# Two 16-head attentions of a layered network: heads in groups side by side, outputs turned, smaller decay tables

## The chip, the cores and the metric

The kernel runs on one core of one Trainium2 chip. The metric is the device time of one execution in microseconds (us). The kernel before takes 3792.23 us, the median of three runs (3791.14 to 3802.96).

## The reference

The network has four levels of self attention, cross attention and feed forward, twelve stages on x (4 batches, 256 tokens, 256 channels, float32), each `x = x + stage(layernorm(x))`. The change rewrites the first two stages.

The first attention is linear attention over 16 heads of 16 channels, with a decay per head, in chunks of 128 tokens:

```python
D = jnp.exp(ld[:, None, None] * jnp.where(mask, diff, 0)) * mask
q_decay = jnp.exp(ld[None, :] * (idx + 1)[:, None])
k_decay = jnp.exp(ld[None, :] * (chunk - 1 - idx)[:, None])
scores = jnp.einsum('bchd,bshd->bhcs', qb, kb) * D[None]
o_intra = jnp.einsum('bhcs,bshd->bchd', scores, vb)
o_inter = jnp.einsum('bchd,bhde->bche', qb, S) * q_decay[None, :, :, None]
```

q, k and v are silu(x W). The output times the sigmoid of a gate (x Wg1 Wg2) is normalised per head by its root mean square, multiplied by norm_w and by Wo. The first cross attention has 16 heads of 16 channels too, keys and values from a latent of 64 channels, a causal mask over 256 x 256 and a softmax.

## The kernel before, in words

A stage is a run of blocks; in a block each engine has its own list of instructions, they wait for each other through semaphores, and a block ends in a barrier. `layernorm` (L203) turns the normalised x into xnT, with channels down the partitions. `refine_rsqrt` (L185) makes one Newton step of four VectorE instructions; all 12 layer norms use it, and two stages. `load` (L314) issues loads on the SyncE queue in the order of its list, and `wait_weights` waits for all loads of one name. A float32 matmul of 128 rows appears in the trace as two records of TensorE (PE) and two weight loads (PEld); a transpose as one.

`l0_attn` (L331) has four blocks. The first (L360 to L461) loads everything under one name and waits for it, then projects q, k and v into PSUM banks: 12 steps through six banks, then the gate's two products. ScalarE takes tanh or silu, VectorE finishes q and k, with q kept twice, once with the odd heads cleared (L425) and once with the even ones (L424), so that 32 rows of k (two heads) can meet one head of q. After that ScalarE makes the table of decays, Exp per head at L457 and Ln at L460, and VectorE corrects it (L430, L433), squares it three times (L435 to L437) and masks it (L438): 16 heads x 384 columns = 6144.

The second block has a loop over 4 x 16 heads. Per head TensorE makes scores in two matmuls of 32 rows (L476 with 256 columns, L478 with 128) and, two heads later, the sums over keys in three matmuls with 128 x 128 weights and 16 columns:

```python
nc.tensor.matmul(o[:, 0, cols], p[:, 0:P], v[:, 2 * b, cols], start=True, stop=True)
nc.tensor.matmul(o[:, 1, cols], p[:, 2 * P:3 * P], v[:, 2 * b + 1, cols], start=True, stop=False)
nc.tensor.matmul(o[:, 1, cols], p[:, P:2 * P], v[:, 2 * b, cols],
```

VectorE multiplies scores by the table (L507). The third block normalises over all tokens at once (L525 to L535, refined at L532), and `project_out` (L256) transposes the result and multiplies it by Wo.

`l0_xattn` (L545) projects in its first block (L579 to L605) and then loops over 32 pairs of heads: scores (L626, L628), mask added by VectorE (L672), maxima (L677 to L679), Exp with its sum on ScalarE (L719), six transposes (L638), a copy (L686), and the sums over keys in 12 records of 16 columns (L651 to L653); `project_out` ends it.

Three other places serve for comparison. In the three latent cross attentions L1569 makes scores with 64 rows for j = 0 and 1 in rows 0 to 63 and 64 to 127, and L1591 writes its results to PSUM partitions 0 to 63 and 64 to 127 in turn; L1579 transposes. In the last self attention L2268 makes scores with 32 rows, two for each of two neighbouring groups of 32 rows. L1223 belongs to the second level's attention.

## Time and profile before

| | |
|---|---|
| profiled execution | 3792.42 us |
| its span in the profile | 3790.2 us |
| TensorE busy | 2875.6 us, 76% |
| VectorE busy | 1894.3 us, 50% |
| ScalarE busy | 1018.8 us, 27% |
| GpSimd busy | 780.8 us, 21% |
| DMA | 73.06 MB, 19 GB/s over the span |
| mean granted TensorE clock | 0.782 of full speed |

The clock is given as a share of 2.4 GHz; 0.50 is 1.2 GHz. The busy shares are means over twelve stages with different limits, so they say little about the two stages at hand; those are read from stretches of time. Column "(x)" counts instructions.

### The profile page before, as it was taken

The numbers are of one execution on the slowest core, as the hardware profiler recorded it, in microseconds if no ns is written. First come the engines' busy times: TensorE is split into PE (matmuls) and PEld (weight loads), VectorE is DVE, ScalarE is ACT, GpSimd is POOL, SyncE is SP. The second block draws the span as 40 slices with busy tenths as digits, with TensorE's granted clock in tenths as the row PEclk, the third lists the DMA queues.
The fourth block names the chain that finished last, engine by engine and source line by source line (L and its number), as shares of the span: only waits on it lengthen the run. The fifth ranks groups of instructions, "written<-read, shape, count | busy, mean of one in ns | idle before, by whom it ended". The sixth has DMA issues, their size and how long they took to land. (4 is left out here: it accounts for less than half of the span.)

```text
span 3790.2 us, 37772 instructions
## 1 busy us (share of the span) xinstructions
PE 2875.6 (76%) x14229; PEld 1963.0 (52%) x14230; DVE 1894.3 (50%) x3700; ACT 1018.8 (27%) x2426; POOL 780.8 (21%) x531
## 2 busy tenths in 40 slices
PE   4596995343649999977768787875999665599799
PEld 2485884221223335555566666664555644455455
DVE  3523444586953345533657575753355645155521
ACT  3000321011520025511233334331355201045411
POOL 0000002000210038821100000000487000068522
PEclk8556555555759999988778787877899875699999
DMA  1000000000020000012000000003000000300211
GB/s 38 0 1 15 1 1 28 5 0 3 0 82 0 0 1 1 1 46 84 18 12 12 12 12 12 12 12 78 1 1 1 34 16 1 78 1 1 64 46 42
DMA packets 95934, 73.06 MB, mean 19 GB/s; under 512 B 50672, under 2 KB 89249, under 8 KB 95178
## 3 DMA queue, kind: packets, MB, share of 16 engines
q1 hardware_dynamic: 94729, 69.20, 6.5%
q8 instruction: 114, 1.87, 0.2%
q0 software_dynamic: 1024, 1.45, 0.1%
q14 instruction: 67, 0.54, 0.0%
HBM read 65.35 MB, written 5.28 MB: 19 GB/s over the span
## 5 line engine op out<-in xcount | busy, mean ns | idle before, releaser
L1688 POOL TENSOR_SCALAR work<-work,small 128x512 f32<-128x512 f32 x384 | 593.1, 1562 | 999.4 <-DVE small L1624 999.4
L1666 ACT ACTIVATE work<-psum,small 128x512 f32<-128x512 f32 x384 | 260.3, 683 | 252.1 <-DVE small L1619 252.1
L1619 DVE TENSOR_REDUCE small<-psum 128x2 f32<-128x1024 f32 x192 | 234.9, 1225 | 179.3 <-PE psum L1569 179.3
L1569 PE MATMUL psum<-keysT,arena_a 64*128 64x512 f32 x768 | 218.9, 648 | 9.1 <-ACT work L1666 6.2
L1579 PEld LDWEIGHTS psum<-consts,work 128*128 128x128 f32 x1536 | 165.9, 141 | 113.5 <-issue 103.6
L1591 PE MATMUL psum<-work,keys 128*64 128x256 f32 x1536 | 186.9, 384 | 36.9 <-issue 34.1
L1579 PE MATMUL psum<-consts,work 128*128 128x128 f32 x1536 | 211.8, 281 | 3.2 <-DVE work L1630 2.6
L1591 PEld LDWEIGHTS psum<-work,keys 128*64 128x64 f32 x1536 | 120.0, 136 | 136.8 <-issue 110.8
L2482 PE MATMUL psum<-xnT,arena_a 128*128 128x256 f32 x512 | 153.6, 461 | 29.6 <-DVE arena_b L2862 29.6
L1223 PE MATMUL psum<-arena_b,arena_a 96*96 96x512 f32 x128 | 95.5, 918 | 71.1 <-DVE arena_b L1252 36.7
L2482 PEld LDWEIGHTS psum<-xnT,arena_a 128*128 128x128 f32 x512 | 116.6, 235 | 56.0 <-DVE arena_b L2862 31.7
L798 POOL DMA_INDIRECT arena_a<-in_down_table,arena_a x8 | 9.8, 1230 | 635.6 <-DMA arena_a<-in_down_index 633.4
L1630 DVE COPY work<-psum 128x512 f32<-128x512 f32 x192 | 130.9, 682 | 19.7 <-PE psum L1579 19.7
L1503 DVE TENSOR_TENSOR arena_a<-psum,work 96x512 f32<-96x512 f32 x96 | 62.8, 680 | 146.0 <-PE psum L1470 146.0
L1673 ACT ACTIVATE work<-psum 128x512 f32<-128x512 f32 x192 | 114.3, 595 | 74.7 <-PE psum L1579 74.7
L2455 POOL TENSOR_TENSOR work<-arena_b 128x512 f32<-128x512 f32 x32 | 33.3, 1039 | 435.1 <-ACT arena_b L2743 401.9
L476 PE MATMUL psum<-arena_a,work 32*128 32x256 f32 x128 | 76.7, 709 | 59.5 <-PEq L72 59.5
L2038 PE MATMUL psum<-xnT,arena_b 128*128 128x512 f32 (+1 forms) x272 | 121.8, 602 | 0.0
L1470 PE MATMUL psum<-xnT,arena_b 128*96 128x512 f32 x256 | 117.3, 601 | 1.6 <-PEq L72 1.6
L1259 POOL TENSOR_TENSOR arena_b<-arena_b 96x1024 f32<-96x1024 f32 x16 | 37.6, 2349 | 380.2 <-DVE arena_b L1252 380.2
L1481 PE MATMUL psum<-arena_a,arena_b 96*64 96x512 f32 x256 | 115.7, 598 | 0.0
L507 DVE TENSOR_TENSOR arena_a<-psum,arena_a 128x384 f32<-128x384 f32 x64 | 35.7, 558 | 148.9 <-PE psum L491 146.2
(558 smaller groups left out, 5891.5 us busy)
## 6 DMA issues: line engine op xcount, KB each, us to landing
arena_a<-in_L_xattn_Wo SPq DMA_DIRECT2D x3, 2048.0 KB, 12.2
arena_a<-in_L_xattn_Wq SPq DMA_DIRECT2D x3, 2048.0 KB, 14.6
arena_a<-in_L_xattn_w_kc_q SPq DMA_DIRECT2D x3, 1536.0 KB, 19.7
arena_a<-in_L_attn_w_qkv SPq DMA_DIRECT2D x1, 4096.0 KB, 12.7
arena_a<-in_L_xattn_W_qr SPq DMA_DIRECT2D x3, 768.0 KB, 4.4
arena_b<-in_L_ffn_w_fc SPq DMA_DIRECT2D x1, 2048.0 KB, 8.9
arena_b<-in_L_ffn_w_proj SPq DMA_DIRECT2D x1, 2048.0 KB, 13.9
arena_a<-in_L_attn_w_gate SPq DMA_DIRECT2D x1, 2048.0 KB, 17.2
```

Source lines behind the costliest of these rows:

```text
L1470: mm = nc.tensor.matmul(ps[0:QH, m % 2 * 2 + q, :], Em[:, c, 2 * i + j, q * QH:(q + 1) * QH], xnT[:, c, n * 512:(n + 1) * 512], start=c == ...
L1481: mm = nc.tensor.matmul(ps[j * DC:(j + 1) * DC, 4 + g % 4, :], Cm[:, c_at(2 * i + j), z // 2, :], prods[m % 2][:, z, :], start=z == 0, sto ...
L1569: mm = nc.tensor.matmul(ps[:, u % 2 * 2 + j, :], qT[r:r + DC, p, t * P:(t + 1) * P], k.keysT[r:r + DC, b * SK:(b + 1) * SK], start=True, s ...
L1579: mm = nc.tensor.transpose(ps[:, 4 + j, c * P:(c + 1) * P], probs[u % NPB][:, j, c * P:(c + 1) * P], k.c["ident"])
L1591: mm = nc.tensor.matmul(ps[j * DC:(j + 1) * DC, 6, 0:S], k.keys[:, 4 * b + c, :], PT[q % 2][:, j, c], start=c == 0, stop=c == 3)
L1619: nc.vector.tensor_reduce(top[:, 2 * u:2 * u + 2], ps[:, u % 2 * 2:u % 2 * 2 + 2, :], AX.X, ALU.max, negate=True).then_inc(*maxed.up())
L1630: nc.vector.tensor_copy(PT[u // 2 % 2][:, 0, :, u % 2, :], ps[:, 4, :].rearrange("p (c n) -> p c n", c=4)).then_inc(*kept_d.up())
L1666: nc.scalar.activation(probs[u % NPB][:, j, :], ps[:, u % 2 * 2 + j, :], ACT.Exp, bias=top[:, i:i + 1], accum_out=total[:, i:i + 1]).then_ ...
L1673: nc.scalar.activation(PT[u // 2 % 2][:, 1, :, u % 2, :], ps[:, 5, :].rearrange("p (c n) -> p c n", c=4), ACT.Copy).then_inc(*kept_a.up())
L1688: nc.gpsimd.tensor_scalar(probs[u % NPB][:, j, :], probs[u % NPB][:, j, :], total[:, i:i + 1], None, ALU.mult).then_inc(*scaled.up())
L2038: mm = nc.tensor.matmul(ps[0:n_f, 4 + g % 2 * 2 + z, :], gu[:, c, z, i * P:i * P + n_f], xnT[:, c, n * 512:(n + 1) * 512], start=c == 0, s ...
L2482: mm = nc.tensor.matmul(ps[:, n % 3, j * S:(j + 1) * S], w_qkv[:, c, f:f + P], xnT[:, c, b * S:(b + 1) * S], start=c == 0, stop=c == 1)
```

## The change

In both attentions four heads are worked on at a time.

First attention. The tables are one tile of 2320 columns: 16 heads x 128 for tokens of one chunk, 256 for q's decay and 16 for k's, made ahead of the projections on VectorE and ScalarE. What the second chunk gets from the first goes through a state: k is projected once more with tokens down the partitions (two more steps), GpSimd multiplies it and q by their decays, and eight matmuls make the states. A unit of scores (16 of them) is four matmuls of 32 rows and 256 columns, alternating between two row groups, over both chunks and both halves of a pair of heads. The sums over keys are turned: values are the weights (32 columns of a padded v), scores stream through, and four matmuls write to the four groups of 32 PSUM partitions; the state's product stands between the two token tiles' sums. The gate is projected turned too, normalisation goes batch by batch (Square and Sqrt on ScalarE, sums and spreading on TensorE, one reciprocal on VectorE, the Newton step on GpSimd) and the output product follows in the same loop; the separate third block and `project_out` are gone. norm_w is multiplied into Wo by GpSimd.

Cross attention. Weights are widened to 32 columns per head (GpSimd copies), so that q and k come out in four groups of four heads. The mask is added by bfloat16 matmuls with an identity. Scores are made twice: once with queries down the partitions, for the maxima; these are turned and subtracted by way of a spare row of q; then with keys down the partitions, so that Exp's result streams straight into the sums, whose 17th row is the softmax's sum. The sums are transposed back and divided. Loads: six instead of five.

`refine_rsqrt` has five instructions instead of four. Constants `dist_mask` and `causal` go, and `tri`, `steps`, `blocks`, `heads8`, `hide` and `one_row` come. The names under which weights are loaded change in all stages, without another effect.

```diff
-    k.link(dve, nc.vector.tensor_tensor(t, r, r, ALU.mult), "dve")
-    k.link(dve, nc.vector.tensor_tensor(t, t, v, ALU.mult), "dve")
-    k.link(dve, nc.vector.tensor_scalar(t, t, -0.5, 1.5, ALU.mult, ALU.add), "dve")
-    k.link(dve, nc.vector.tensor_tensor(r, r, t, ALU.mult), "dve")
+    k.link(dve, nc.vector.tensor_tensor(t, r, v, ALU.mult), "dve")
+    k.link(dve, nc.vector.tensor_tensor(t, t, r, ALU.mult), "dve")
+    k.link(dve, nc.vector.tensor_scalar(t, t, -0.5, 0.5, ALU.mult, ALU.add), "dve")
+    k.link(dve, nc.vector.tensor_tensor(t, t, r, ALU.mult), "dve")
+    k.link(dve, nc.vector.tensor_tensor(r, r, t, ALU.add), "dve")
...
+    TQ, TK, TN = H * P, H * P + 2 * P, H * P + 2 * P + H
+    arg, powers, logs = A.take(P, TN), A.take(P, TN), A.take(P, TN)
+    table = powers[:, 0:TQ].rearrange("p (h n) -> p h n", h=H)
+    q_decay = powers[:, TQ:TK].rearrange("p (e n) -> p e n", e=2)
+    k_decay = powers[:, TK:TN]
...
+            load(k, sp, "third", [(ld, io["L0_attn_log_decay"].rearrange("(o h) -> o h", o=1).broadcast_to([P, H])),
+                                (heads8, k.const("heads8")), (dist, k.const("dist")), (steps, k.const("steps")),
+                                (tri, k.const("tri"))])
+            load(k, sp, "first", [(wq, interleaved(io["L0_attn_Wq"])), (wk, interleaved(io["L0_attn_Wk"])),
                                 (wv, interleaved(io["L0_attn_Wv"])), (wg1, interleaved(io["L0_attn_Wg1"])),
-                                (wg2, io["L0_attn_Wg2"]), (wo, rows(io["L0_attn_Wo"])),
-                                (ld, io["L0_attn_log_decay"].rearrange("(o h) -> o h", o=1).broadcast_to([P, H])),
-                                (norm_w, io["L0_attn_norm_w"].rearrange("(o h) -> o h", o=1).broadcast_to([P, D]))]
-                 + [(d, k.const(n)) for d, n in ((dist, "dist"), (dmask, "dist_mask"))])
+                                (wg2, io["L0_attn_Wg2"])])
+            load(k, sp, "second", [(wo, rows(io["L0_attn_Wo"])), (blocks, k.const("blocks"))])
...
+            def scores(u):
...
+                if u >= 2:
+                    pe.wait_ge(*decayed.at(u - 1))
+                for t in range(2):
+                    cols = slice((2 * b + t) * P, (2 * b + t + 1) * P)
+                    for j in range(2):
+                        r = 64 * half + 32 * j
+                        mm = nc.tensor.matmul(ps[:, u % 2 * 2 + j, t * 2 * P:(t + 1) * 2 * P], kT[r:r + 32, e, cols],
+                                              q2[r:r + 32, :, e, cols], start=True, stop=True)
+                mm.then_inc(*scored.up())
...
+                def own(t, par):
+                    for r in range(4):
+                        mm = nc.tensor.matmul(o[32 * r:32 * r + 32, t * P:(t + 1) * P],
+                                              v[:, 2 * b + t, 4 * e + r, 16 * par:16 * par + 32],
+                                              probs[(2 * s + r // 2) % 4][:, r % 2, t, par, :],
+                                              start=t == 0 and par == 0, stop=par == 1, skip_group_check=True)
+                    return mm
+                own(0, 0)
+                own(0, 1)
+                nc.tensor.matmul(o[:, P:S], state[:, s, :], qd[:, e, b, :], start=True, stop=False, skip_group_check=True)
+                own(1, 0)
+                own(1, 1).then_inc(*valued.up())
...
+                for t in range(2):
+                    for e in range(2):
+                        c = t * H + e * 8
+                        mm = nc.tensor.matmul(ps[:, 7, c:c + 8], sq[:, e, t * P:(t + 1) * P], heads8, start=True, stop=True)
+                mm.then_inc(*summed.up())
...
+                for e in range(2):
+                    for t in range(2):
+                        mm = nc.tensor.matmul(ps[:, 6, e * S + t * P:e * S + (t + 1) * P], rs[:, t, e * P:(e + 1) * P],
+                                              k.c["ident"], start=True, stop=True)
+                mm.then_inc(*spread.up())
...
+                for t in range(2):
+                    for e in range(2):
+                        mm = nc.tensor.matmul(ps[:, 7, t * D:(t + 1) * D], out_n[:, e, t * P:(t + 1) * P], wo[:, e, :],
+                                              start=e == 0, stop=e == 1)
+                mm.then_inc(*outd.up())
...
+            for s in range(2 * B + 4):
+                if s < 2 * B:
+                    scores(2 * s)
+                b, odd = divmod(s - 3, 2)
+                if odd == 0 and 0 <= b < B:
+                    sums(b)
+                if odd == 1 and 0 <= b < B:
+                    output(b)
+                if s < 2 * B:
+                    scores(2 * s + 1)
+                if 1 <= s <= 2 * B:
+                    values(s - 1)
+                if odd == 0 and 0 <= b < B:
+                    spread_out(b)
...
+            act.wait_ge(*decays.at(1))
+            k.link(act, nc.scalar.activation(powers, arg, ACT.Exp, scale=0.125), "act")
+            nc.scalar.activation(logs, powers, ACT.Ln, bias=k.c["tiny"]).then_inc(*k.sig("logs").up())
...
+            for b in range(B):
+                act.wait_ge(*gated.at(b + 1))
+                if b >= 1:
+                    act.wait_ge(*summed.at(b))
+                nc.scalar.activation(sq, og, ACT.Square).then_inc(*squared.up())
+                act.wait_ge(*summed.at(b + 1))
+                if b >= 1:
+                    act.wait_ge(*refined.at(b))
+                    act.wait_ge(*inverted.at(b))
+                k.link(act, nc.scalar.activation(mean, ps[:, 7, 0:32], ACT.Identity, bias=k.c["eps5"], scale=1.0 / HD), "act")
+                nc.scalar.activation(root, mean, ACT.Sqrt).then_inc(*rooted.up())
...
+            nc.gpsimd.tensor_tensor(qd, q.rearrange("p e (b n) -> p e b n", b=B)[:, :, :, P:S],
+                                    q_decay.unsqueeze(2).broadcast_to([P, 2, B, P]), ALU.mult)
...
+            nc.gpsimd.tensor_tensor(k0h, k0h, k_decay.unsqueeze(1).unsqueeze(3).broadcast_to([P, B, H, HD]),
+                                    ALU.mult).then_inc(*kept_k.up())
...
+                k.link(pool, nc.gpsimd.tensor_tensor(half_step, root, root, ALU.mult), "pool")
+                k.link(pool, nc.gpsimd.tensor_tensor(half_step, half_step, mean, ALU.mult), "pool")
+                k.link(pool, nc.gpsimd.tensor_scalar(half_step, half_step, -0.5, 1.5, ALU.mult, ALU.add), "pool")
+                nc.gpsimd.tensor_tensor(rs.rearrange("p t (h d) -> p (t h) d", d=HD),
+                                        root.unsqueeze(2).broadcast_to([P, 2 * H, HD]),
+                                        half_step.unsqueeze(2).broadcast_to([P, 2 * H, HD]), ALU.mult).then_inc(*refined.up())
...
+            dve.wait_ge(*k.sig("logs").at(1))
+            k.link(dve, nc.vector.scalar_tensor_tensor(out=arg, in0=arg, scalar=0.125, in1=logs, op0=ALU.mult,
+                                                       op1=ALU.subtract), "dve")
+            k.link(dve, nc.vector.scalar_tensor_tensor(out=powers, in0=arg, scalar=1.0, in1=powers, op0=ALU.add,
+                                                       op1=ALU.mult), "dve")
+            k.link(dve, nc.vector.tensor_tensor(powers, powers, powers, ALU.mult), "dve")
+            k.link(dve, nc.vector.tensor_tensor(powers, powers, powers, ALU.mult), "dve")
+            nc.vector.tensor_tensor(powers, powers, powers, ALU.mult).then_inc(*k.sig("decay_done").up())
+            dve.wait_ge(*k.sig("decay_done").at(1))
+            nc.vector.tensor_scalar(k_decay, k_decay, 0.5, None, ALU.mult).then_inc(*k.sig("decay_done").up())
+            k.link(dve, nc.vector.scalar_tensor_tensor(out=table, in0=table, scalar=SCALE, in1=tri.unsqueeze(1).broadcast_to(
+                [P, H, P]), op0=ALU.mult, op1=ALU.mult), "dve")
...
+                nc.vector.tensor_tensor(probs[u % 4].rearrange("p j t g n -> p j t (g n)"),
+                                        ps[:, u % 2 * 2:u % 2 * 2 + 2, :].rearrange("p j (t n) -> p j t n", t=2),
+                                        own.unsqueeze(2).broadcast_to([P, 2, 2, 2 * P]), ALU.mult).then_inc(*decayed.up())
...
+            def masked(bank, kind):
+                nc.tensor.matmul(ps[:, bank, 0:3 * P].rearrange("p (a n) -> p a n", a=3)[:, 0:3:2, :], ident16, hide16[:, kind],
+                                 start=True, stop=False, skip_group_check=True)
...
+                for j in range(2):
+                    masked(2 * w + j, 0)
+                t0 = b * S
+                for a, e in ((0, 1), (1, 3)):
+                    for j in range(2):
+                        r = 64 * half + 32 * j
+                        mm = nc.tensor.matmul(ps[:, 2 * w + j, a * P:e * P], qT[r:r + 32, g, t0 + a * P:t0 + (a + 1) * P],
+                                              kT[r:r + 32, g, t0:t0 + (a + 1) * P], start=False, stop=True,
+                                              skip_group_check=True)
+                mm.then_inc(*scored.up())
...
+                for t in range(2):
+                    mm = nc.tensor.transpose(ps[:, 7, t * P:(t + 1) * P], tops[s % 2][:, t, :], k.c["ident"])
...
+                for j in range(2):
+                    masked(2 * w + j, 1)
+                t0 = b * S
+                for a, e in ((0, 2), (2, 3)):
+                    for j in range(2):
+                        r = 64 * half + 32 * j
+                        t = a // 2
+                        mm = nc.tensor.matmul(ps[:, 2 * w + j, a * P:e * P], kT[r:r + 32, g, t0 + t * P:t0 + (t + 1) * P],
+                                              low_q[s % 2][r:r + 32, t * P:S], start=False, stop=True, skip_group_check=True)
+                mm.then_inc(*rescored.up())
...
+                for t in range(2):
+                    for r in range(4):
+                        mm = nc.tensor.matmul(ps[32 * r:32 * r + 32, 6, t * P:S], v[:, 2 * b + t, 4 * g + r, :],
+                                              probs[(2 * s + r // 2) % 4][:, r % 2, 2 * t * P:(2 + t) * P],
+                                              start=t == 0, stop=t == 1, skip_group_check=True)
...
+            for s in range(Q + 2):
+                if s < Q:
+                    scores(s, 0)
+                if 1 <= s <= Q:
+                    turn_tops(s - 1)
+                if s >= 2:
+                    values(s - 2)
+                if 1 <= s <= Q:
+                    scores_again(s - 1, 0)
+                if s < Q:
+                    scores(s, 1)
+                if s >= 2:
+                    turn_sums(s - 2)
+                if 1 <= s <= Q:
...
+                for t in range(2):
+                    c = 64 * half + 16
+                    last = nc.vector.tensor_reduce(tops[s % 2][:, t, c:c + 33:32], ps[:, 2 * w:2 * w + 2, t * P:(2 * t + 1) * P],
+                                                   AX.X, ALU.max, negate=True)
...
+                nc.vector.tensor_tensor(low_q[s % 2], ps[:, 7, 0:S], qT[:, g, b * S:(b + 1) * S], ALU.add).then_inc(*lowered.up())
...
+                nc.scalar.activation(probs[u % 4], ps[:, 2 * w:2 * w + 2, 0:3 * P], ACT.Exp, scale=SCALE).then_inc(*expd.up())
...
+                nc.scalar.activation(sums[s % 2], ps[:, 6, 0:S], ACT.Copy).then_inc(*kept.up())
...
```

## Rows read from the trace of the kernel before

**Rows 1.** Stretches of both stages: busy us of PE, PEld, DVE, ACT, POOL, clock
```profile
35.30:79.30 44.00, 33.49 (x88) 18.16 (x88) 11.25 (x21) 15.80 (x23) 0.00 (x0) 0.93 0.13 37
79.30:137.30 58.00, 0.00 (x0) 0.00 (x0) 41.34 (x21) 16.39 (x21) 0.00 (x0) 0.50 0.00 0
137.30:326.50 189.20, 187.98 (x640) 159.99 (x640) 38.19 (x69) 0.00 (x0) 0.00 (x0) 0.50 0.00 0
326.50:350.60 24.10, 10.82 (x48) 9.61 (x48) 15.58 (x16) 2.88 (x4) 0.00 (x0) 0.66 0.00 0
...
361.10:386.60 25.50, 16.43 (x40) 8.23 (x41) 0.00 (x0) 9.76 (x17) 0.00 (x0) 0.80 0.23 55
386.60:601.90 215.30, 212.24 (x831) 184.50 (x832) 99.54 (x169) 60.85 (x257) 0.00 (x0) 0.50 0.00 1
```

**Rows 2.** Timeline, one head, first loop: start us, length us, operation.
```profile
144.97 1.22 PE L476 MATMUL psum<-arena_a,work 32*128 32x256 f32 x2
...
145.98 0.63 PE L478 MATMUL psum<-arena_a,work 32*128 32x128 f32 x2
...
146.54 0.61 PE L489 MATMUL psum<-work,arena_a 128*128 128x16 f32 x2
...
147.42 0.59 PE L491 MATMUL psum<-work,arena_a 128*128 128x16 f32 x2
...
147.93 1.22 PE L476 MATMUL psum<-arena_a,work 32*128 32x256 f32 x2
```

**Rows 3.** Timeline, six transposes of a pair in the second loop.
```profile
504.49 1.54 PE L638 MATMUL psum<-consts,work 128*128 128x128 f32 x6
```

**Rows 4.** Timeline of later stages: matmuls of neighbouring groups in a row.
```profile
1504.74 1.13 PE L1569 MATMUL psum<-keysT,arena_a 64*128 64x512 f32 x4
...
1506.26 1.95 PE L1591 MATMUL psum<-work,keys 128*64 128x256 f32 x16 [0.39 <-issue]
...
3173.04 2.08 PE L2268 MATMUL psum<-arena_b 32*128 32x256 f32 x8
```

**Rows 5.** Stretches, same columns: stages of lines 1223, 1569 and 2268.
```profile
1050.00:1060.00 10.00, 8.52 (x13) 2.51 (x12) 9.82 (x10) 6.31 (x6) 3.80 (x2) 0.67 0.00 0
...
1500.00:1600.00 100.00, 94.91 (x602) 57.76 (x599) 59.56 (x98) 53.55 (x135) 83.51 (x55) 1.00 0.00 1
...
3170.00:3180.00 10.00, 6.26 (x26) 4.77 (x28) 4.72 (x16) 2.04 (x8) 0.00 (x0) 0.50 0.00 0
```

**Rows 6.** Timeline: the first projection of the stage.
```profile
43.33 17.03 PE L386 MATMUL psum<-xnT,arena_a 128*128 128x512 f32 x32 [8.79 <-DMA arena_a<-in_consts]
```

**Rows 7.** Groups, first 420 us: xcount, busy us, mean ns, idle before.
```profile
L433 DVE SCALAR_TENSOR_TENSOR arena_a<-arena_b,arena_a 128x6144 f32<-128x6144 f32 x1 | 6.6, 6559 | 0.0
...
L460 ACT ACTIVATE arena_b<-arena_a,consts 128x6144 f32<-128x6144 f32 x1 | 5.4, 5414 | 0.0
...
L457 ACT ACT_TABLE_LOAD x1 | 1.3, 1283 | 0.0
...
L525 DVE TENSOR_TENSOR arena_a<-work 128x2048 f32<-128x2048 f32 x1 | 2.3, 2293 | 0.3 <-PEq L72 0.3
...
L427 DVE COPY work<-psum 16x1024 f32<-16x1024 f32 x1 | 1.2, 1214 | 2.5 <-PE psum L398 2.5
```

**Rows 8.** Groups by line and form; the first two from the first 420 us.
```profile
L672 DVE TENSOR_TENSOR work<-psum,arena_b 128x768 f32<-128x768 f32 x6 | 5.7, 956 | 40.7 <-PE psum L628 40.7
...
L678 DVE TENSOR_REDUCE small<-work 128x2 f32<-128x512 f32 x6 | 4.1, 675 | 0.0
...
L2455 POOL TENSOR_TENSOR work<-arena_b 128x512 f32<-128x512 f32 x32 | 33.3, 1039 | 435.1 <-ACT arena_b L2743 401.9
...
L1259 POOL TENSOR_TENSOR arena_b<-arena_b 96x1024 f32<-96x1024 f32 x16 | 37.6, 2349 | 380.2 <-DVE arena_b L1252 380.2
```

**Rows 9.** Timeline: two steps of the refinement in a layer norm.
```profile
355.39 0.17 DVE L190 TENSOR_SCALAR ln_rs<-ln_rs 128x8 f32<-128x8 f32 x1
355.59 0.17 DVE L191 TENSOR_TENSOR ln_rs<-ln_rs 128x8 f32<-128x8 f32 x1
```

720 lines of the change are left out of this document (386 added, 334 removed).

## The prediction

> **What bounds the kernel now.** First I read the table of stretches. The two stages that the change rewrites run from 35.3 to 350.6 us and from 361.1 to some 616. Their loops over the heads, 189.2 and 215.3 us, have TensorE busy for 99% of the time, at a granted clock of 0.50; ahead of the first loop lie 58.0 us without one matmul [rows 1]. So TensorE's own work ends each head, and VectorE (38.2 us of 189.2) only follows. Second, the timeline of one head shows what that work is. Head after head starts 2.96 us apart (144.97 to 147.93). A float32 matmul leaves two records: 256 columns give two of 0.43 us, 128 columns two of 0.21 us, and a matmul of only 16 columns takes as long as one of 128, since two loads of 128 columns of weights stand before it: the six records of lines 489 to 491 take 1.28 us [rows 2]. In units for 1.2 GHz: 0.85 us for 256 columns, 0.43 us for 128 columns or for a weight load alone, half of it at 2.4 GHz. A head is 0.85 + 0.43 + 3 x 0.43 = 2.56, and 0.4 us goes in two changes of the array's shape: 0.2 us each. A transpose leaves one record, 0.21 us (six in 1.54 us, the last 0.2 being latency) [rows 3]. A pair of the second loop is 2.56 + 1.28 + 2.56 = 6.4, and 215.3/32 = 6.73 is measured: the units hold. Both stages lie on the path, for each stage starts after a barrier.
>
> **What side by side is worth.** The third view is of later stages. Line 2268 has exactly the new scores' shape, four matmuls of 32 rows and 256 columns in two row groups: eight records in 2.08 us at clock 0.50, where one after another would be 3.41. Line 1569 (two row groups, 512 columns) gives four records in 1.13 us, not 1.71. Line 1591 (two column groups, 256 columns) gives sixteen in 1.95 us, not 3.4 at 2.4 GHz [rows 4, 5]. Two groups thus run at once; four column groups, as in the new value sums, no row shows.
> The Trainium skill (TensorEngine Tiling (Array Packing), Key Properties) says that a change of tiling mode drains TensorE, which speaks against nine such changes per group; the 0.2 us above is what this trace has for it, so the sum already carries it.
>
> **Attention, up to its loop: 102 us now.** Ten loads still stand before the first matmul, so it starts at 43.3 as now [rows 6]. The table shrinks from 6144 to 2320 columns. Arguments: 2.3 for 2048 columns and some 1 for small ones, from about 41 to 44.6. Exp and Ln: 2320/6144 x 5.41 = 2.0 each and a table load of 1.28, to 50.0. Five VectorE passes (first step, correction, three squarings) of 2320/6144 x 6.56 = 2.48 make 12.4, plus the mask 2.3 and 0.3: 65. All of it now stands ahead of taking q, and TensorE's seventh projection waits for a bank that this frees: it has had nothing to do since 52 and goes on at 65.8 [rows 7]. ScalarE's tanh and silu queue behind Exp and Ln, but have caught up by then. The tables' five small loads now stand first on SyncE's queue; Wo and norm_w come last, needed only late. From there, at 1.72 per bank (4 records of 512 columns at 2.4 GHz): 8 banks 13.8, restart at 1.2 GHz 3.4, gate 3.4, copy of 16x1024 1.4, gate's second product 3.4, eight state products 1.7: loop start at 92.9 for 137.3, 44.4 saved. GpSimd's new work (1024 columns twice, 2.35 each) ends near 85 and is covered; uncovered, it would cost 2 to 5 us.
>
> **Attention's loop and end: 213.3 us now.** Per batch at 1.2 GHz: scores 16 matmuls in pairs 6.8; values 32 in fours and 2 state products, 8 x 0.43 + 2 x 0.43 = 4.3; sums 4 x 0.43, spread 4 x 0.43, output 4 x 0.85: 6.8; ten changes 2.0. That is 20, and 10.5 at 2.4 GHz. Waits: at 2.4 GHz the chain sums, Sqrt 0.7, reciprocal 0.4, GpSimd 2.1 (one of 512 columns is 1.04), spread is longer than scores and values beside it by 1.4, and gating 0.7 and Square 0.6 leave 1.1: 13 per batch. VectorE has 4 x 1.23 (1024 columns, from 0.96 for 768) + 2.4 = 7.3 per batch and doesn't bound [rows 8]. The last batch's chain and the fill add 9. So 89 at 1.2 GHz and 61 at 2.4; at the average I take, 67: 146 saved.
>
> **Cross attention.** Projection: q in four groups 8 x 1.72, k 8 x 0.86, v 4 x 0.86 = 24.0, 4.3 for the restart, 10.2 of loads and GpSimd widening before: 38.5 for 25.5. Loop, 16 groups of four heads, at 1.2 GHz: 8 bfloat16 mask products of 256 columns at one pass, 1.7; two times scores in pairs, 4 x 1.28 = 5.1; four transposes 0.85; values in fours 1.28; nine changes 1.5: 10.5. At 2.4 GHz 4.5 + 1.2, and 1.0 because VectorE's maxima (0.4 + 0.68) and lowering (0.4) with their latencies are longer than the 1.1 beside them: 6.7. VectorE 3.1 and ScalarE 2.2 per group fit [rows 1, 8]. The loop is 168 or 107, at my average 119; fill and drain 5. With 240.8 now for both parts: 78 saved.
>
> **Elsewhere.** The rsqrt refinement has one more VectorE step, 0.20 us from start to start, in 12 layer norms and once in another stage: +2.6 [rows 9]. Renamed semaphores: nothing. The unseen four column groups: if only two run at once, values cost twice as much, 14 + 20 us at 1.2 GHz and 17 at 2.4; if four do, nothing. Nearest are the rows for two [rows 4]; I take 10.
> Sum: 44.4 + 146 + 78 - 2.6 - 10 = 256 us off the profiled execution's 3792.4, which lies 0.2 us from the median: 3536.
>
> **The clock** is the largest unknown. The old loops sit at 0.50; so does the stage of line 2268, with TensorE busy 6.3 of 10 us; the stage of lines 1569 and 1591 sits at 1.00, and that of line 1223 changes between the levels, mean 0.67 [rows 1, 5]. The new loops are between these: pairs and fours, short waits. I take about 0.8 of full speed.
>
> **Rivals.**
> (a) *Half clock in both loops*, as now. For it: the old loops. Against: full columns now stream where 16 did. 44.4 + (213.3 - 89) + (240.8 - 211.5) - 2.6 = 195, or 161 with two column groups at once: 3597 to 3631.
> (b) *Full clock throughout*: 44.4 + 152 + 90 - 2.6 = 284: 3508. The Trainium skill (TensorE: Matmul & The Clock Gate, HAM oscillation) has the clock fall only where TensorE idles, which would give this; the old loops, 99% busy at 0.50, contradict it here [rows 1].
> (c) *Slower: nothing runs side by side in float32 with these neighbours*, in both loops, at 1.2 GHz. Scores 13.7 and values 14.5 per batch: 37, so the first loop and end are 157 and attention saves 101. Cross attention: 1.7 + 10.2 + 0.85 + 5.1 + 1.5 = 19.4 per group, 310, and with 43.5 some 354: 113 lost. In all +15: 3807. It decides only if almost all overlap is missing; [rows 4] speak against it.
> (d) *It doesn't do what it says*: "three squarings" are there before too, and the gain might end in the new chain of waits through GpSimd. Then about 3790; VectorE and GpSimd would have to take 200 us more than their rows give.
>
> **Numbers.** Forecast 0.55, (a) 0.25, (b) 0.16, (c) 0.03, (d) 0.01. The range 3495 to 3605 holds the forecast, (b) and the near end of (a). A measurement of this kernel tells about 0.3%, 11 us, from no change: faster 0.96, within 0.01, slower 0.03.
>
> **What would show it.** A unit of scores near 2.0 us at clock 0.5 or 1.1 at 1.0; value fours whose eight records take 0.43 or 0.21 us and not twice that; the loops' clock; attention ending near 170 and not 350; some 14 us without a matmul after 52; waits on GpSimd once per batch. Wrong it would be if the four groups queue, if the clock stays at 0.50, or if VectorE's waits fill the new loops.

## The result and the profile after

The changed kernel takes **3549.6 us** (median of four runs: 3534.7, 3545.2, 3554.0 and 3572.0), 0.936 of the time before (95% interval 0.931 to 0.941). The forecast was 3536 and the range 3495 to 3605: 13.6 us off, 0.4%. The profiled execution is the longest of the four, 3572.0, and is compared with the 3792.4 of the one before. An execution more than 1.5% above the fastest of its kernel is left out of the medians and ratios below (3760.7 us of six with cross attention alone, 3554.6 of four with the four-row order on two row groups).

The page's busy times of the changed kernel:

```profile
PE 2707.2 (76%) x14214; PEld 1752.2 (49%) x14214; DVE 1797.3 (50%) x3596; ACT 981.6 (27%) x2209; POOL 800.4 (22%) x565
```

The table of stretches of the changed kernel. A line has the stretch and its length in us, then for PE, PEld, DVE, ACT and POOL the busy us and in brackets the instructions, then the granted clock, the DMA share and GB/s. The stretches are: attention up to its loop; its loop and end; cross attention's loads and widening; its projections; its loop at either clock.

```profile
35.90:98.10 62.20, 43.30 (x112) 23.29 (x112) 27.79 (x27) 21.45 (x29) 7.28 (x5) 0.74 0.08 22
98.10:164.60 66.50, 56.57 (x497) 39.72 (x496) 29.73 (x34) 5.87 (x13) 7.04 (x16) 0.76 0.00 1
...
175.50:184.30 8.80, 0.00 (x0) 0.01 (x1) 0.00 (x0) 0.00 (x0) 1.84 (x5) 0.65 0.59 149
184.30:211.60 27.30, 26.52 (x64) 12.74 (x65) 5.53 (x8) 7.99 (x13) 3.46 (x9) 0.92 0.00 0
...
211.60:362.00 150.40, 149.54 (x810) 81.68 (x810) 39.16 (x96) 26.83 (x39) 0.00 (x0) 0.50 0.00 1
362.00:380.60 18.60, 15.49 (x154) 9.35 (x151) 5.63 (x16) 6.39 (x10) 0.00 (x0) 0.96 0.01 1
```

Attention's loop and end went from 213.3 us to 66.5 and its start from 102.0 to 62.2. Cross attention's loop went from 215.3 us [rows 1] to 169.0, and in 150.4 of these TensorE was busy for 99% of the time at a granted clock of 0.50, as it was in all of the old loop. The clock then rose to 1.00 and the last groups ran at it. The four executions lie 37 us apart. Only one of them has a trace, but three kernels with this same loop have one each, and in these the clock rises 103, 126 and 151 us after the loop's start (below); I put the spread down to that.

The timeline of the attention loop: start us, length us, operation. The `x8` of scores (L451) are a unit of four float32 products in two row groups, the `x16` of value sums (L465) eight products in four column groups.

```profile
113.48 2.08 PE L451 MATMUL psum<-arena_a,work 32*128 32x256 f32 x8
115.48 1.08 PE L465 MATMUL psum<-arena_b,work 128*32 128x128 f32 x16
...
124.27 0.64 PE L465 MATMUL psum<-arena_b,work 128*32 128x128 f32 x16
...
125.84 1.13 PE L451 MATMUL psum<-arena_a,work 32*128 32x256 f32 x8
...
137.78 0.43 PE L465 MATMUL psum<-arena_b,work 128*32 128x128 f32 x8
```

A unit of scores takes 2.08 us at 1.2 GHz and 1.13 at 2.4. Sixteen records of value sums, two fours of 128 columns, take 1.08 and 0.64: two times 0.43 or 0.21 us and the latency behind, where eight products in a row would be 3.4 or 1.7 by the prediction's units (an estimate). A batch starts 13.5 us after the last (124.27 to 137.78).

One group of cross attention in the same trace, from one pair of transposes (L765) to the next:

```profile
304.77 0.69 PE L765 MATMUL psum<-consts,work 128*128 128x128 f32 x2
305.39 1.51 PE L794 MATMUL psum<-work,arena_a 128*32 128x256 f32 x16
306.83 0.61 PE L741 MATMUL psum<-arena_b 128*128 128x256 bf16 x2
307.37 1.65 PE L783 MATMUL psum<-work,arena_a 32*128 32x256 f32 x8
308.95 0.61 PE L741 MATMUL psum<-arena_b 128*128 128x256 bf16 x2
...
315.81 0.69 PE L765 MATMUL psum<-consts,work 128*128 128x128 f32 x2
```

11.05 us a group at 1.2 GHz, without a gap. Before every unit of scores stand its two mask products (L741), which use all 128 rows.

Ahead of the attention loop, the timeline of the changed kernel around the end of the table passes:

```profile
66.57 6.13 PE L405 MATMUL psum<-xnT,arena_a 128*128 128x512 f32 x7 [10.10 <-DVE arena_b L613]
...
69.98 0.48 DVE L617 TENSOR_SCALAR arena_a<-arena_b,consts 128x512 f32<-128x512 f32 x1
...
71.09 0.49 DVE L616 TENSOR_SCALAR arena_a<-arena_b,consts 128x512 f32<-128x512 f32 x1
71.21 2.58 POOL L567 TENSOR_TENSOR work<-arena_b,arena_a 128x1024 f32<-128x1024 f32 x1 [25.04 <-DVE arena_b L613]
71.49 2.58 DVE L617 TENSOR_SCALAR arena_a<-arena_b,consts 128x512 f32<-128x512 f32 x1
```

And TensorE's last two products ahead of the loop, by the timeline of TensorE alone:

```profile
88.33 6.15 PE L424 MATMUL psum<-arena_b,arena_a 16*128 16x512 f32 x8 [1.31 <-DVE arena_b L619]
94.41 3.78 PE L430 MATMUL psum<-work 128*128 128x128 f32 x16
```

TensorE stands still for 10.1 us until VectorE has taken the first bank of q, and its clock is back at 0.50 when it goes on. The clock rises again beside the projections. After a second wait, of 1.31 us for the gate's copy, it falls once more: of the 6.15 us most, and all of the 3.78, ran at 1.2 GHz (granted clock 0.68 from 88 to 92 us, 0.50 from 92 to 96). And the same VectorE instruction (L617, 128x512) takes 0.48 us alone and 2.58 us where GpSimd's product L567 runs beside it, to about the moment when that ends (71.21 + 2.58).

### The profile page after: what moved, and what is told of

Same layout as the page of the kernel before. It is cut to its first block and busy times, and to the rows that moved or that the text cites. A ratio compares the mean times of both kernels' runs of the same rounds, so it can differ in the third digit from the quotient of the medians.

```text
span 3570.2 us, 37436 instructions
## 1 busy us (share of the span) xinstructions
PE 2707.2 (76%) x14214; PEld 1752.2 (49%) x14214; DVE 1797.3 (50%) x3596; ACT 981.6 (27%) x2209; POOL 800.4 (22%) x565
## 5 line engine op out<-in xcount | busy, mean ns | idle before, releaser
L251 PE MATMUL psum<-consts,xn 128*128 128x128 f32 x192 | 44.1, 423 | 87.0 <-DVE xn L232 87.0
L3064 DVE SCALAR_TENSOR_TENSOR work<-psum,conv_w,work 128x255 f32<-128x255 f32 (+2 forms) x192 | 83.1, 476 | 37.9 <-ACT work L2939 35.3
L1803 PE MATMUL psum<-arena_b,work 128*128 128x256 f32 x384 | 99.1, 381 | 1.6 <-DVE work L1839 1.6
```

## The experiments

Ratios are to the kernel before, timed on the same chip.

**One stage at a time.** Attention changed, cross attention as before: the constants for the old one come back.

```diff
+    low = np.where(j <= i, 0.0, NEG)
+    c["causal"] = np.concatenate([low, np.zeros((P, P)), low], 1)
```

> Only the linear attention and the five-step refinement are new; the cross attention is that of the kernel before. Theory (the gain is the sum of two stages that don't touch each other, and only the new cross attention's loop has an unsteady clock): the attention stage takes 315.2 us before and 128.7 after, so 3792 - 186.5 + 2.4 = 3608, and the executions lie within some 5 us. Rival (the spread of the changed kernel comes from the attention's loop, whose clock is the unsteady one): 3600 to 3640 and a spread of 20 us or more.

Measured: 3612.0 us, ratio 0.951 (0.950 to 0.953), four runs within 7.2 us. It saves 182.8 us.

And cross attention changed, attention as before:

```diff
-    c["dist"], c["tri"] = np.maximum(j - i, 0), j >= i
+    same, cross = j - i, P + j - i
+    c["dist"] = np.concatenate([np.maximum(same, 0), cross, np.maximum(same, 0)], 1)
```

> Only the cross attention and the refinement are new. Theory: the stage takes 255 us before and 217.5 in the profiled execution of the changed kernel, where the granted clock of its loop was 0.50 nearly to the end: 3757 if it stays there, down to 3700 where the clock rises early; the spread of the changed kernel (37 us between executions) comes back here. Rival (the clock of this loop is set by what the attention ahead of it did): the loop's clock is another than in the changed kernel and the executions agree within 5 us.

Measured: 3708.0 us, ratio 0.977 (0.974 to 0.979); the six runs lie between 3704.7 and 3760.7, three of them at 3705 to 3708 and three at 3741 to 3761. Its loop in the table of stretches:

```profile
399.70:522.00 122.30, 121.42 (x656) 66.56 (x658) 32.17 (x79) 22.07 (x32) 0.00 (x0) 0.51 0.00 1
522.00:558.80 36.80, 33.12 (x306) 19.46 (x304) 12.64 (x34) 11.23 (x17) 0.00 (x0) 0.92 0.01 1
```

The spread thus belongs to cross attention, and in this profile (3740.7 us) its clock rose some 126 us after the loop's start, against 151 in the changed kernel's. Cross attention alone saves 34 to 90 us by execution, 87 by the median. With 182.8 that would be 270 us, where both together gave 243. So the gains add within cross attention's spread, and no more closely than that is shown.

**VectorE takes q ahead of the table.** The passes over the table are moved behind the taking of q, and the copy of the gate's product goes ahead of the last squaring.

```diff
+            for i in range(4):
+                e, cols = i // 2, slice(i % 2 * 512, (i % 2 + 1) * 512)
+                dve.wait_ge(*tanhed.at(i + 1))
...
             dve.wait_ge(*k.sig("logs").at(1))
```

> The changed kernel, but VectorE takes q (four banks) before it corrects and squares the decays, and copies the gate's first product between the squarings. Theory (the 10.1 us without a matmul after 56.5 are VectorE's table passes standing ahead of the bank that the seventh projection needs): this stall goes, the loop starts near 83 for 98.1 us, and 12 to 15 us are saved. Rival (the tables are needed just as late, by GpSimd's products of q and k, so the wait only moves): the state products wait for GpSimd instead, loop start at 95 or later, less than 4 us saved.

Measured: 3553.0 us, ratio 0.938 (0.934 to 0.942): no difference from the changed kernel can be told, since cross attention's clock moves the time by more. The stages' own times tell it. The timeline of this kernel ahead of its loop:

```profile
74.46 1.21 DVE L614 COPY arena_b<-psum 16x1024 f32<-16x1024 f32 x1 [5.65 <-PE psum L418]
...
78.27 2.28 DVE L618 SCALAR_TENSOR_TENSOR arena_a<-arena_a 128x2048 f32<-128x2048 f32 x1
78.45 4.31 POOL L567 TENSOR_TENSOR work<-arena_b,arena_a 128x1024 f32<-128x1024 f32 x1 [31.99 <-DVE arena_a L617]
...
84.70 3.78 PE L430 MATMUL psum<-work 128*128 128x128 f32 x16 [2.52 <-POOL work L571]
88.41 1.38 PEld L451 LDWEIGHTS psum<-arena_a,work 32*128 32x128 f32 x16 [0.23 <-issue]
```

The loop starts at 88.4 and not 98.1. These 9.7 us lie between the 12 to 15 of the theory and the 4 of the rival: the wait of 10.1 us goes, and the rival is right for a part. VectorE now waits 5.65 us for the gate's product before its last squaring, GpSimd's product waits for that, and TensorE waits 2.52 us for GpSimd, whose product starts beside VectorE's mask pass and takes 4.31 us for 2.58.

**Scores over four row groups.** In cross attention the second scores of one half and the first scores of the other half go out together: first the four masks, then eight products in turns over four row groups and four banks; the sums' transposes get the other half of bank 7, so that they need not wait. The waits and the order of VectorE's and ScalarE's work move with it, so this is more than a change of width.

```diff
+            def joint(*pieces):
+                for w, kind, _, _ in pieces:
+                    for j in range(2):
+                        masked(2 * w + j, kind)
+                for n in range(2):
+                    for _, _, part, done in pieces:
+                        for j in range(2):
+                            mm = part(n, j)
```

> The changed kernel, with the cross attention's second scores of one half and the first scores of the other half interleaved, so that four row groups and four PSUM banks are in use at a time (masks of both ahead of them); turning and sums move between them. Theory (row groups overlap up to four, TensorE's own work is what ends each group): 7.4 us of work and 0.5 of waits per group at 1.2 GHz for 11.05, 50 us saved; if the clock then goes to 2.4 GHz 4.9 us per group and 97 us saved. Rival (only two groups run at once, or loads of weights are the limit): a group takes 10 us or more at 1.2 GHz, at most 17 us saved. Second rival (the chain of maxima, lowering and Exp ends each group): idle times of TensorE of 2 us and more per group, 8 to 9 us each at either clock.

Measured: **3488.6 us**, ratio 0.919 (0.917 to 0.921), four runs within 7.3 us. Its loop in the table of stretches:

```profile
211.40:225.00 13.60, 12.09 (x74) 7.59 (x74) 4.42 (x9) 2.15 (x3) 0.00 (x0) 0.52 0.01 2
225.00:302.00 77.00, 66.32 (x888) 43.23 (x886) 40.40 (x103) 31.04 (x47) 0.00 (x0) 1.00 0.01 2
```

And half a group in its timeline:

```profile
246.49 0.48 PE L778 MATMUL psum<-work,arena_a 32*128 32x256 f32 x2
246.50 0.48 PE L753 MATMUL psum<-arena_a 32*128 32x256 f32 x2
...
247.35 0.44 PE L811 MATMUL psum<-consts,work 128*128 128x128 f32 x2
248.41 0.60 PE L741 MATMUL psum<-arena_b 128*128 128x256 bf16 x4 [0.62 <-ACT work L895]
```

Two units run in some 0.9 us, where at the same clock one unit alone takes 0.92 (line 783 of the kernel with one column group, below). A group takes 5.01 us (242.34 to 247.35, start to start of L811), near the 4.9 that were expected at this clock, and the clock is at 1.00 some 14 us after the loop's start, although TensorE is busy for 86% and not 99%. The loop's 91 us against 169 come from both: 16 groups x (6.5 - 5.0) = 24 us are of the shorter group, the rest is clock (estimates). Of these 24, some 17 are the width of four row groups and some 6 the new order, by the kernel with the same order and two row groups below.

**Mask products in float32.**

```diff
-                nc.tensor.matmul(ps[:, bank, 0:3 * P].rearrange("p (a n) -> p a n", a=3)[:, 0:3:2, :], ident16, hide16[:, kind],
+                nc.tensor.matmul(ps[:, bank, 0:3 * P].rearrange("p (a n) -> p a n", a=3)[:, 0:3:2, :], k.c["ident"], hide[:, kind * P:(kind + 1) * P].unsqueeze(1).broadcast_to([P, 2, P]),
```

> Cross attention's mask products take a float32 identity and float32 mask rows over all 128 rows of the array instead of bfloat16 ones; same values. In the changed kernel a pair of them takes 0.61 us at 1.2 GHz, four pairs a group of 11.05 us. As float32 a pair should take about 1.9 us at 1.2 GHz and 1.0 at 2.4. Theory A (the clock of this loop rises when more of the work that the engine takes in is wide float32 work, and the bfloat16 masks and narrow score pairs hold it down): the loop runs at 1.00 from its start, a group takes 6.5 + 2.6 = 9.1 us, the loop 146 us against 168.5, the kernel about 3530 with a spread of under 10 between runs. Theory B (the clock has nothing to do with what is multiplied): 0.50 for most of the loop, a group 16.2 us, 82 us more, about 3630.

Measured: 3557.9 us, ratio 0.938 (0.936 to 0.939), four runs within 18.3 us. Its loop in the table of stretches:

```profile
211.00:238.00 27.00, 26.16 (x88) 15.57 (x88) 4.91 (x11) 2.61 (x3) 0.00 (x0) 0.50 0.00 1
238.00:376.00 138.00, 132.21 (x999) 86.01 (x998) 39.35 (x100) 30.48 (x46) 0.00 (x0) 0.99 0.00 1
```

A group takes 9.36 us at 2.4 GHz, 2.9 more than with bfloat16 masks, and yet the whole is no longer: the clock rose about 30 us into the loop and gave back all that the masks cost. Neither theory had this: A expected 1.00 from the loop's start and 3530 us, B 0.50 and 3630.

**One row group for each pair of heads**, in both loops.

```diff
-                        r = 64 * half + 32 * j
+                        r = 64 * half
```

> Every score product of both attention loops that belongs to the second head of a pair reads the row group of the first head, so that the two of a pair can't lie side by side; the scores of every second head are those of its neighbour. Nothing else differs. Theory (two row groups work at once): the attention loop's unit of eight records goes from 1.13 to about 2.0 us at 2.4 GHz and from 2.08 to 3.6 at 1.2, and cross attention's from 0.92 to 1.7 and from 1.65 to 3.1: 16 units give 14 to 24 us and 64 units 50 to 93 us, together 64 to 117 over the changed kernel's median, so 3615 to 3670, less if the clock rises earlier. Rival (the products of two row groups were taking turns anyway, and the gain came from elsewhere): units unchanged and 3550.

Measured: 3688.6 us, ratio 0.973 (0.971 to 0.974): 139 us more than the changed kernel, 117 at most expected. Its timeline, one unit of either loop and a pair of transposes of the second:

```profile
119.97 3.78 PE L451 MATMUL psum<-arena_a,work 32*128 32x256 f32 x8
...
250.85 2.92 PE L783 MATMUL psum<-work,arena_a 32*128 32x256 f32 x8
...
360.72 0.69 PE L765 MATMUL psum<-consts,work 128*128 128x128 f32 x2
```

A unit goes from 2.08 to 3.78 us and from 1.65 to 2.92, at 1.2 GHz. A group is 16.1 us (344.58 to 360.72), and the clock stayed at 0.50 to the end of the loop, 262 us: that is what was not expected.

**One column group for the value sums**, in both loops.

```diff
-                        mm = nc.tensor.matmul(ps[32 * r:32 * r + 32, 6, t * P:S], v[:, 2 * b + t, 4 * g + r, :],
+                        mm = nc.tensor.matmul(ps[0:32, 6, t * P:S], v[:, 2 * b + t, 4 * g + r, :],
```

> All four heads' value sums of a group write column group 0 instead of groups 0 to 3, in both loops; the four results fall into the same rows and the other rows are left as they are. Theory (four column groups work at once): sixteen records of the attention loop take 1.08 us at 1.2 GHz and 0.64 at 2.4; one column group alone gives eight products of 128 columns one after the other, 1.8 us at 2.4 and 3.5 at 1.2, sixteen times: 19 to 39 us; cross attention's sixteen records go from 1.51 to 5.2 us at 1.2 and from 0.86 to 2.6 at 2.4, sixteen groups: 28 to 59 us. Together 47 to 98 us over the changed kernel, 3597 to 3648. Rival (only two column groups work at once, the allowance of 10 us of the prediction): half of that. Rival (they take turns): no change, 3550.

Measured: 3554.8 us, ratio 0.937 (0.936 to 0.939), four runs within 4.8 us. By the total the rival would have it; the timeline refutes it:

```profile
242.63 4.94 PE L794 MATMUL psum<-work,arena_a 128*32 128x256 f32 x16
...
252.84 2.79 PE L794 MATMUL psum<-work,arena_a 128*32 128x256 f32 x16
...
255.88 0.92 PE L783 MATMUL psum<-work,arena_a 32*128 32x256 f32 x8
```

The sixteen records take 4.94 us for 1.51 at 1.2 GHz and 2.79 for 0.86 at 2.4, so four column groups do work at once in the changed kernel. And the stretches of this kernel's loop show where the loss went:

```profile
226.00:245.00 19.00, 18.13 (x80) 9.40 (x81) 5.78 (x12) 2.81 (x3) 0.00 (x0) 0.51 0.00 1
245.00:366.00 121.00, 119.59 (x879) 74.17 (x877) 38.49 (x98) 30.10 (x45) 0.00 (x0) 0.99 0.00 1
```

The clock rose about 20 us into the loop: groups of 8.06 us at 2.4 GHz in place of 11.05 at 1.2. The loop is 142 us, 27 less than the changed kernel's in its profile; attention, whose value sums are longer too, takes 14 of these back (the loop starts at 226.0 and not 211.6).

**The order of the four-row kernel with two row groups.** Both halves read the row groups of the first.

```diff
-                    r, t0 = 64 * half + 32 * j, b * S
+                    r, t0 = 32 * j, b * S
...
-                    r, t0, t = 64 * half + 32 * j, b * S, a // 2
+                    r, t0, t = 32 * j, b * S, a // 2
```

> As the kernel with four row groups, in the same order and with the same banks, but the scores of the two halves, issued in turns, read the same two row groups, so that two work at once and not four; the second half's scores are those of the first half's heads. This tells the width from the order. Theory W (the clock of this loop rises when more of the array works at once): the loop falls back to 0.50 for most of its length, groups of 10 to 11 us, and the kernel to 3530 to 3575 with a spread of over 20 us between runs. Theory O (it is the order, with the short pauses that the wait for GpSimd-free buffers and ScalarE leaves in every group, that lets the clock rise): the loop stays at 1.00 from 220 us on, a group takes the 5.0 us of four row groups plus about 1.6, and the kernel 3488 + 16 x 1.6 = 3514, spread under 10.

Measured: 3507.5 us, ratio 0.925 (0.922 to 0.927); three runs at 3499 to 3512 and one at 3554.6. Its loop:

```profile
211.80:236.00 24.20, 21.80 (x138) 14.41 (x140) 8.15 (x17) 4.77 (x6) 0.00 (x0) 0.65 0.01 2
236.00:318.00 82.00, 76.33 (x818) 53.73 (x818) 36.12 (x93) 28.11 (x42) 0.00 (x0) 1.00 0.01 1
```

Its groups take 6.09 us, 1.1 more than with four row groups (1.6 were expected) and 0.4 less than the changed kernel's at the same clock, and the clock is at 1.00 from about 24 us into the loop. So four row groups aren't needed for the clock to rise early: something in the order does it, as theory O had it. The fourth run, 47 us longer than the profiled one and without a trace, may be one in which it rose late; the spread of under 10 us that O expected didn't come. TensorE's wait in this kernel is 0.41 us and comes once a group, not twice as the expectation of the next run has it.

**A pause in every group of the changed kernel**, to tell pauses from order.

```diff
+                if s >= 1 and half == 1:
+                    pe.wait_ge(*expd.at(2 * (s - 1) + 1))
```

> The changed kernel with one wait more in cross attention: in every group TensorE holds back the scores of the second half until ScalarE has taken the exponentials of the first half of the group before. Same products in the same order; TensorE should stand still for about 1.0 us in each group (0.81 us of ScalarE and the way there and back). Theory O (with pauses in its groups the loop's clock rises early, as it did in the kernel with the interleaved order and two row groups, which had 0.41 us twice a group): 1.00 within 40 us of the loop's start, groups of about 7.5 us, the loop 130 us against 168.5 in the changed kernel's profile, the kernel about 3530 with a spread under 15. Theory P (the pauses have nothing to do with it, it is which products follow one another): 0.50 as long as before, groups of 12 us while it lasts, about 3565 with a spread over 20.

Measured: 3587.4 us, ratio 0.947 (0.944 to 0.949). Timeline of the pause, and then the stretches of the loop:

```profile
265.11 0.59 PE L741 MATMUL psum<-arena_b 128*128 128x256 bf16 x2 [1.00 <-ACT work L893]
```

```profile
210.00:320.00 110.00, 100.00 (x552) 55.04 (x552) 26.69 (x65) 18.82 (x27) 0.00 (x0) 0.53 0.00 1
320.00:331.00 11.00, 10.00 (x64) 5.24 (x62) 3.19 (x9) 2.00 (x3) 0.00 (x0) 0.66 0.00 1
331.00:400.00 69.00, 61.97 (x347) 33.91 (x346) 14.69 (x40) 12.40 (x19) 0.00 (x0) 0.50 0.00 1
```

There is a pause of 1.00 us in every group, groups take 12.1 us, and the clock stayed at 0.50 but for the first 7 us and a part of one group. This pause doesn't lift it, as theory P had it. The time is 22 us above P's 3565, since here the clock never rose for good.

**The order of the four-row kernel, half by half.** Masks in fours as there, but then all products of one half before those of the other.

```diff
-                for n in range(2):
-                    for _, _, part, done in pieces:
+                for _, _, part, done in pieces:
+                    for n in range(2):
```

> As the kernel with four row groups, but behind the four masks the products of one half come all before those of the other, as in the changed kernel, so that two row groups work at once and four only where one half's last product meets the other's first. Order of the steps, banks, masks in fours and the waits stay. It tells the interleaving from the rest of the new order, of which the kernel with two row groups interleaved ran 1.00 from about 238 us. Theory I (the taking in turns of products of equal size keeps the array fuller and that lets the clock rise early): without it the loop stays at 0.50 for most of its length, groups of about 11 us, the kernel 3540 to 3575 with a spread over 20. Theory M (the rest of the order does it: masks in fours, short pauses behind them): 1.00 within 40 us of the loop's start, groups of 6.0 to 6.5 us, the kernel 3500 to 3515.

Measured: 3493.8 us, ratio 0.920 (0.919 to 0.922), four runs within 11.6 us. The timeline of one unit, and the stretches of the loop:

```profile
256.40 0.48 PE L778 MATMUL psum<-work,arena_a 32*128 32x256 f32 x2
256.43 0.48 PE L753 MATMUL psum<-arena_a 32*128 32x256 f32 x2
256.72 0.38 PE L778 MATMUL psum<-work,arena_a 32*128 32x256 f32 x2
256.75 0.38 PE L753 MATMUL psum<-arena_a 32*128 32x256 f32 x2
```

```profile
215.00:237.00 22.00, 19.01 (x124) 11.80 (x126) 7.42 (x16) 4.22 (x5) 0.00 (x0) 0.50 0.00 1
237.00:308.00 71.00, 62.95 (x838) 41.67 (x830) 37.00 (x95) 28.45 (x43) 0.00 (x0) 0.99 0.01 2
```

Neither theory had all of this. The clock went as M says, but four row groups still work at once: the second half's products (L753) start 0.03 us after the first half's (L778), although four matmuls of the first half stand ahead of them in the program. The order in which the eight products are written costs nothing (a group of 5.03 us against 5.01). So what keeps the halves apart in the changed kernel is something else: probably the masks and transposes over all 128 rows that stand between them. That isn't isolated, since the places of the semaphore waits moved together with the masks.

**Both improvements together**: q first, and four row groups.

```diff
+            joint(scores(0, 0))
+            for s in range(Q + 3):
+                pieces = ([scores_again(s - 1, 0)] if 1 <= s <= Q else []) + ([scores(s, 1)] if s < Q else [])
...
+            dve.wait_ge(*low.at(1))
+            nc.vector.tensor_copy(t1.rearrange("p (a b) -> p a b", a=2), ps[0:HD, 6:8, :]).then_inc(*put.up())
```

> The two versions together: VectorE takes q ahead of the table's long passes (loop start 88.4 us instead of 98.1) and cross attention's scores go over four row groups. Cross attention's clock is no longer in play, since with four row groups it rose within 15 us of the loop's start in the profiled run and the four runs lie within 7 us. Theory (the two savings add, the stages follow one another on TensorE): 3488.6 - 9.7 = 3479, spread under 10. Rival (what attention saves is given back, because the gap between the stages is set by the layer norm and by the widening of the weights on GpSimd, whose end waits for the loads): 3486 to 3489.

Measured: **3480.2 us**, ratio 0.918 (0.917 to 0.920), five runs over 14 us. Its cross attention loop starts at 201.7 for 211.4, so the 9.7 us are kept from stage to stage, and the medians are 8.4 us apart where 9.7 were expected; but the intervals of the two ratios overlap, so the total alone doesn't show it. It beats the kernel before by 313 us and the changed kernel by 69.

**The cross attention loops beside each other**, from the profiled executions (length from the first mask to the output projection's first matmul; a group from start to start of its first pair of transposes; one execution each):

| kernel | group at 1.2 GHz | group at 2.4 GHz | clock up after | loop us |
|---|---|---|---|---|
| changed | 11.05 | - | 151 | 169.0 |
| q first | 11.05 | 6.49 | 103 | 146.8 |
| pause | 12.1 | - | one group only | 190.5 |
| one row group | 16.1 | - | never | 261.7 |
| float32 masks | - | 9.36 | 30 | 166.6 |
| one column group | - | 8.06 | 20 | 141.9 |
| four-row order, two row groups | - | 6.09 | 24 | 108.4 |
| four-row order, by half | 7.4 | 5.03 | 24 | 95.2 |
| four row groups | - | 5.01 | 14 | 91.0 |

## Why the prediction was right, and where it was off

**What bounds.** Right: both loops were TensorE's, and putting groups side by side shortened them. The chains through VectorE, ScalarE and GpSimd cost TensorE waits of under a microsecond inside the loops, but for 1.4 us at the start of attention's and 1.5 and 3.1 us in its last batch.

**Up to attention's loop: 92.9 forecast, 98.1 measured** (62.2 us of stage for 57.6). TensorE restarted at 66.6 for 65.8. It had gone idle at 56.5 and not at 52, so the gap was 10.1 us and not some 14, which changes nothing in the sum. The rest is two terms: the gate's second product and the state products, costed at 2.4 GHz with 3.4 and 1.7 us, took 6.15 and 3.78, since the clock had fallen again when they came: 4.8 us. GpSimd's product, which I had called covered, is so here; its delay of VectorE's L617 by 2.1 us lies beside TensorE's projections. With q taken first it is no longer covered and costs the 2.5 us of TensorE's wait that the prediction had put at 2 to 5. The idle time I took as given, where another order of VectorE's work removes it.

**Attention's loop and end: 67 forecast, 66.5 measured.** A batch takes 13.5 us at mostly 2.4 GHz for 13, and most of the first batch and of the last chain ran at 1.2 GHz, mean 0.76. Scores in pairs and values in fours came out as costed. TensorE waits for GpSimd in the last batch alone, 3.1 us; in the other three GpSimd's product ends before TensorE needs it, so the sign "waits on GpSimd once per batch" didn't come. That 67 fits so well is in part luck: a mean clock of 0.76 over the time would make some 72 us out of the prediction's 61 and 89 (an estimate).

**Cross attention's projections: 38.5 forecast, 36.1 measured.**

**Cross attention's loop: 119 + 5 forecast, 169 measured** in the profiled execution. This is the step that failed. A group is 11.05 us at 1.2 GHz for 10.5, and 6.49 at 2.4 for 6.7; the units were right. The assumed clock wasn't: "I take about 0.8 of full speed" was used for both loops alike, and is near attention's (0.76), but cross attention's loop ran at 0.50 for 150 us, a mean of 0.55. For this loop rival (a) was nearly the true one (168 + 5), and only for this loop; it differs in that groups are longer and the last 19 us ran at 0.96. The step from the clock to the sum was off as well: 67 and 119 us are what comes out when a fifth of the work runs at 1.2 GHz, which is a mean clock over the time of some 0.86. A mean of 0.8 would give some 70 and 125 us, and a forecast of 3545 (estimates).

**The allowance of 10 us** for only two column groups at once, which no row of the kernel before bore out or spoke against, wasn't needed: four work at once, as the experiment with one column group shows.

**Elsewhere**: 2.6 us for the refinement; the stages end 223.1 us earlier (393.0 for 616.1) and the span is 220.0 shorter, so 3.1.

Summed: 5.2 - 0.5 - 2.4 + 45 - 10 = 37 us over the forecast in the profiled execution, which is 36 us over. The other three runs are 18 to 37 us shorter than the profiled one; one lies below the forecast. So the median came within 14 us partly by luck: two errors, a clock too high for one loop and an allowance too many, have opposite signs, and where the clock rises differs by execution.

**The rivals.** (a) as a whole (3597 to 3631) is refuted by the time, and by attention's clock. (b), full clock throughout, is refuted by cross attention's 150 us at 0.50. The Trainium skill (TensorE: Matmul & The Clock Gate, HAM oscillation) has the clock fall where TensorE idles. That leaves these 150 us unexplained: TensorE waited 0.78 and 0.84 us at the loop's start, and not at all from 220 to 362 us. The four-row kernel's 77 us at 1.00 with TensorE busy 86% of the time aren't a second case against it, since its single waits are 0.62 us, but they show that the busy share doesn't put these loops in order. (c) is refuted by the timelines: with one row group per pair a unit takes 1.8 times as long, with one column group 3.3 times. (d), no gain, is refuted by the time.

**What stays open** is why cross attention's clock rises when it does. In every profile of the new loop the clock is at 1.00 in the projections before it and falls within the loop's first 8 us (in the changed kernel 1.00 from 205 to 210, 0.50 from 215). Whether it rises again soon depends on what TensorE is given: float32 masks, value sums one after another, and masks in fours with the scores together all bring it up 14 to 30 us into the loop, while the changed kernel's order needs 103 to 151 us, with a pause per group it gets there for a part of one group alone, and with one row group never. Each kernel has one profile, so for the early ones too this is one execution each; their runs lie 5 to 18 us apart, but for the one of 3554.6. Two kernels, one with more work and one with less of it side by side, took no clearly longer time for that reason. No single property that sorts all nine loops was isolated.

## What to carry to other kernels

When narrow matmuls are put side by side, look at what stands between the units. Here two units with a product over all 128 rows between them ran one after the other, and with all such products collected ahead of both they ran at once, whatever the order inside them. Judge an edit to a TensorE-bound loop by its units' durations at a known clock and by the loop's granted clock, never by the total alone, as the column group experiment would have read "no effect". And do not carry one mean clock from loop to loop: give each loop its own two cases.

## What was not expected of the hardware

- A loop may sit at 1.2 GHz with TensorE always busy (150 us at 0.50), and its clock may rise in mid-loop with nothing changed in its instructions. Executions of one kernel differ by 37 and 56 us, probably for it: between the profiles of the changed kernel and of the one with q first, 22 of the 32 us are this loop, by the moment when its clock rises.
- Products of different row groups start together across four matmuls of program order (256.40 and 256.43).
- GpSimd and VectorE delay each other: L617 takes 2.58 us for 0.48 beside GpSimd's L567, and with the order turned round GpSimd's L567 takes 4.31 for 2.58 beside VectorE's mask pass. The Trainium skill (SBUF — State Buffer, SBUF: two separate sides) has a port pair shared by the two, held by one instruction to its end. The trace agrees: in the first case VectorE's instruction ends 0.3 us after GpSimd's. And in both cases GpSimd's ends 2.2 us after the VectorE instruction that ran when it started (L616 ends at 71.58 and L567 at 73.79; the mask pass at 80.55 and L567 at 82.76), so already the 2.58 holds some 0.4 us of waiting.
